# Second layers of expert pairs tile by tile, the last pair's one step later, and eight loads of shared rests

## The chip, the cores and the metric

One core of a Trainium2 chip runs the whole kernel. The metric is the device time of one execution in microseconds (us), here as the median of several runs. TensorE is called PE, VectorE DVE, ScalarE ACT, GpSimd POOL, SyncE SP.

## The reference

2048 rows (2 x 1024) of 256 numbers go through a gated cross attention and then through a mixture of experts:

```
x = x + tanh(g_xattn) * attention(layernorm(x), ctx)
y = layernorm(x)
shared = (sum over 2 of gelu(y @ sw1[s] + sb1[s]) @ sw2[s] + sb2[s]) / 2
gates = y @ router_w + router_b           # 8 experts, the top 2 of each row, softmax of the two
moe = sum over the 2 of prob * (gelu(y @ w1[e] + b1[e]) @ w2[e] + b2[e])     # 256 -> 512 -> 256
out = x + tanh(g_ffn) * (shared + moe)
```

Matrix products keep float32 accuracy: each operand is split into a rounded high part and a rest ("hi", "lo"), and three products are summed: hi x hi, hi x lo, lo x hi.

## The kernel before

Attention, routing and the first six of eight parts of the shared experts take the first 219 us of the span. Then the 4096 (row, expert) entries, sorted by expert, are worked through in 39 tiles of 128 rows (SLOT_TILES). Tiles 0 to 5 are single steps; tiles 6 to 29 are twelve pairs (DOUBLES), each of two tiles of one expert, worked as 256 rows; tiles 30 (SINGLE1) to 38 are single steps again. Last come the two parts of the shared experts that are left (EARLY and LAST) and the sum.

A tile goes through these stations:

- POOL gathers its rows (gather(s), into xsl) by a table of names that SP has loaded, and at the end scatters its result (scatter(s), y_tok). All POOL's DMAs stand in one written order. Behind the pairs it is gather(s + 2), scatter(s - 3) for s = 31, 32, ...; gather(s) also waits for xt_psum(s - 1).
- PE turns the rows (turn, L1458 and L1482), ACT copies the high part (turned, turned_wide), DVE makes the rest (xsT_lo, L2077 and L2089).
- PE does the first layer, here called hidden(s): single tiles 6 matmuls of 512 columns (L1550), pairs 24 of 256 (L1589).
- Single tiles: DVE copies the result out (hs, L2109), PE transposes it (L1574), ACT does the gelu (L1053) and the high part (hr_hi, L1057), DVE the rest (L2083). Pairs come out transposed already, in two halves of the 512 hidden units: gelus(h) (L1066), kept(h) (hr_hi, L1079) on ACT, half_left(h) (L2138) on DVE.
- PE does the second layer: give (12 matmuls, L1469), give_wide (24 matmuls, L1495). ACT takes it out, scaled by the weight of the expert (output, L1025, into ysl).

Every engine has its own written order. In double(s), PE does the first layer of the pair, turns the rows of the next pair, and does the second layer of the pair before: give_wide(s - 2). ACT does gelus(0), turned_wide for the next pair, kept(0), gelus(1), kept(1), and the outputs of tiles s - 2 and s - 1. DVE does b_cur (the bias column), xsT_lo for the next pair, half_left(0), a copy of next weights, half_left(1), another copy of weights. In the pair before the last, bias_weights(EARLY, LAST) stands at the end instead of weight copies.

kept(0) writes the first half of hr2_hi, which give_wide of the pair before reads, so it waits for half_used; kept(1) waits for ye_psum, the end of that give_wide:

```python
elif h == 0:
    act.wait_ge(half_used, s - DOUBLE0)
else:
    act.wait_ge(ye_psum, s)
```

hr_hi and hr_lo of the single tiles lie on the same words: tile 30's hr_hi on the first half of the last pair's. An output waits for the scatter that last used its ysl buffer (y_stored), two tiles earlier.

The rests of the shared experts' weights (sw_lo) were stored to DRAM to make room for w1_cur, the weights of the pairs. SP loads them back behind the last pair, in four pieces of 512 KB, in the loop that also loads the tables of names: at s = 35 to 38 it waits for xt_psum(s - 3), loads the table, and then loads a piece. The weights are wanted again at 353.6 us.

Of the kernel before, what the change touches and what calls it, by code (L numbers as in the profile page):

```python
# [16 lines left out]
F32 = mybir.dt.float32  # L17
# [51 lines left out]
def build(nc, x, ctx, g_xattn, g_ffn, g_x, b_x, g_c, b_c, Wq, Wk, Wv, Wo,  # L69
          router_w, router_b, w1, b1, w2, b2, sw1, sb1, sw2, sb2, out):  # L70
    st = ExitStack()
    with st:
# [376 lines left out]
        def _(sp):  # L449
# [65 lines left out]
            for s in range(SLOT_TILES):  # L515
                n = s % IN_FLIGHT
                if s >= IN_FLIGHT:
                    sp.wait_ge(xt_psum, s - IN_FLIGHT + 1)
                sp.load(regs[n], name_tile[0:1, entry(s):entry(s) + 1])
                row = sp.snap(regs[n], min_val=0, max_val=NAME_TILES - 1)  # L520
                sp.dma_start(table[:, s, :], name_tiles[at(row)].rearrange("a p c -> p (a c)")
                             ).then_inc(table_loaded[n], 16)
                n = s - (SLOT_TILES - BACK)
                if n >= 0:
                    sp.wait_ge(h_psum, SINGLE1 + n)
                    piece = slice(n * 2 * SW_WORDS // BACK, (n + 1) * 2 * SW_WORDS // BACK)
                    sp.dma_start(sw_s[1][:, piece].bitcast(F32), sw_lo_kept[:, piece]).then_inc(sw_moved, 16)

# [251 lines left out]
        def _(act):  # L780
# [253 lines left out]
            def step(s, par):  # L1034
                if s + 1 == DOUBLE0:
                    turned_wide(s + 1, 0)
                elif s + 1 < SLOT_TILES:
                    turned(s + 1, 1 - par)
                else:
                    act.wait_ge(h_psum, SLOT_TILES)  # L1040
                    columns(EARLY, late)
                if s == SINGLE1:
                    output(s - 2, 0)
                    output(s - 1, 1)
                elif s >= 2 and s != SINGLE1 + 1:
                    output(s - 2, par)
# [8 lines left out]
                last.then_inc(ht_raw, 1)  # L1055
                act.wait_ge(ht_raw, s + 1)
                nc.scalar.activation(hr_hi[:, par, :, :], hr[:, :, :], ACT.Copy).then_inc(ht_hi, 1)  # L1057

            def double(d, par, s, j):
# [28 lines left out]
                gelus(1)  # L1088
                kept(1)
                output(s - 2, 0)  # L1090
                output(s - 1, 1)
# [12 lines left out]
        def _(pe):  # L1104
# [381 lines left out]
            def give_wide(s, n):  # L1486

                e = expert(n)
                pe.wait_ge(ye_ready, s)
                for h in range(2):  # L1490
                    pe.wait_ge(ht_lo, s + (h + 1))
                    for t in range(2):
                        for i, (h_part, w_part) in enumerate(((hr2_hi, w2_s[0]), (hr2_hi, w2_s[1]), (hr2_lo, w2_s[0]))):
# [5 lines left out]
                        if h == 1:  # L1499
                            last.then_inc(ye_psum, 1)  # L1500
                    if h == 0:
                        last.then_inc(half_used, 2)

# [34 lines left out]
            def step(s, par):  # L1538
# [16 lines left out]
                if s + 1 < SLOT_TILES:  # L1555
# [3 lines left out]
                    else:  # L1559
                        turn(s + 1, 1 - par)  # L1560
                if s == SINGLE1:
                    give_wide(s - 2, 1)
                elif s >= 2 and s != SINGLE1 + 1:
                    if s == 2:
# [55 lines left out]
            give(SLOT_TILES - 2, SLOT_TILES % 2, SLOT_TILES - 2)  # L1620
            pe.wait_ge(sw_moved, 16 + 16 * BACK)
            hidden(EARLY, late, range(0, 1))
# [9 lines left out]
        def _(dve):  # L1632
# [468 lines left out]

            def step(s, par):

# [4 lines left out]
                dve.wait_ge(h_psum, s + 1)  # L2108
                nc.vector.tensor_copy(hs[:, :], bank[2 + par][:, :]).then_inc(h_ready, 1)  # L2109
                if s + 1 < SLOT_TILES:  # L2110
                    fetch(s + 1, entry(s + 1))
# [21 lines left out]
            def double(d, par, s, j):  # L2133
# [20 lines left out]
                if more:  # L2154
                    dve.wait_ge(h_psum, s + 2)
                    move_weights(par, 0)
                half_left(1)
                if more:
# [67 lines left out]
```

## Time and profile before

| | us |
|---|---|
| median of 3 runs | 384.3 (382.98 to 384.43) |
| the profiled execution: its time, its span | 384.16, 382.4 |
| PE busy | 372.3 (97%) |
| DVE, ACT, POOL busy | 282.1, 242.0, 220.1 |
| first and last second layer of a pair (L1495) | 250.4 and 322.1 |
| granted TensorE clock over the span | 1.000 |

Start times count from the start of the span. In a timeline a row gives start, duration, engine, line, operation, output and inputs, the count, and in brackets how long the engine was idle before it and what ended that. PE's matmuls overlap: a matmul of 256 columns is listed with 0.28 us, and the next starts 0.12 us later.

### The profile page before, as it was taken

How to read it: one execution, taken by the hardware profiler on the slowest of the kernel's cores; microseconds unless marked ns; L12 is line 12 of the kernel's file. 1: busy time of each engine (PE TensorE's matmuls, PEld its weight loads, DVE VectorE, ACT ScalarE, POOL GpSimd, SP SyncE). 2: the span in 40 equal slices, each digit the busy share in tenths (PEclk: the TensorE clock that was granted, in tenths of full speed). 3: DMA queues.
4: the chain of work that ended last, by engine and by line, in shares of the span. 5: the costliest groups of instructions: out<-in, count | busy, mean ns of one | idle time of the engine just before them, and what ended most of it. 6: DMA issues, size and time to landing. Idle time of an engine off the chain costs nothing.

```text
span 382.4 us, 8794 instructions
## 1 busy us (share of the span) xinstructions
PE 372.3 (97%) x2773; PEld 353.1 (92%) x2774; DVE 282.1 (74%) x612; ACT 242.0 (63%) x540; POOL 220.1 (58%) x262
## 2 busy tenths in 40 slices
PE   8999999999999999999999999999999998899996
PEld 7898889999999999999999989999999996779996
DVE  5798799978988988799899886555555653445486
ACT  2777545655664654887869857666666654667850
POOL 8367657688878764477782245566666564543100
PEclk9999999999999999999999999999999999999999
DMA  7990000001000058501950112222232323641397
GB/s 228 312 326 3 2 14 29 16 21 35 14 14 14 29 177 304 236 4 22 270 154 2 27 45 85 71 70 83 83 86 79 98 84 111 195 116 39 99 351 252
DMA packets 33263, 40.15 MB, mean 105 GB/s; under 512 B 9610, under 2 KB 26444, under 8 KB 33100
## 3 DMA queue, kind: packets, MB, share of 16 engines
q1 hardware_dynamic: 28384, 29.40, 24.8%
q0 software_dynamic: 4768, 10.28, 8.8%
q8 instruction: 19, 0.31, 0.4%
q14 instruction: 16, 0.13, 0.2%
q10 hardware_dynamic: 76, 0.02, 0.0%
HBM read 27.88 MB, written 11.68 MB: 103 GB/s over the span
## 4 chain that ended last, share of the span: by engine, by line
PE 85%; DMA 4%; DVE 3%; ACT 3%; issue 3%; POOL 2%; DVEq 0%; ACTq 0%; POOLq 0%
PE psum L1327 12%; PE psum L1350 12%; PE psum L1287 10%; PE psum L1243 9%; PE psum L1589 8%; PE psum L1495 6%; PE psum L1469 5%; PE psum L1550 4%; PE psum L1210 3%; DMA xsl<-y_rows,table 3%; PE psum L1129 2%; PE psum L1167 2%; PE psum L1191 2%; PE psum L1275 1%; PE psum L1482 1%
## 5 line engine op out<-in xcount | busy, mean ns | idle before, releaser
L739 POOL DMA_INDIRECT y_tok<-ysl,table x39 | 39.1, 1002 | 39.6 <-ACT ysl L1025 34.7
L732 POOL DMA_INDIRECT xsl<-y_rows,table x39 | 39.0, 1000 | 37.0 <-PE psum L1458 12.5
L705 POOL DMA_INDIRECT names<-named,pos x32 | 35.5, 1109 | 12.8 <-issue 8.2
L658 POOL TENSOR_TENSOR Eb<-Eb,rinv 128x512 f32<-128x512 f32 x32 | 33.5, 1066 | 13.1 <-DVE rinv L1801 13.1
L1066 ACT ACTIVATE hr<-psum,b_cur 128x256 f32<-128x256 f32 x48 | 20.2, 472 | 22.1 <-DVE b_cur L2094 12.3
L901 ACT ACTIVATE yTb<-psum 128x256 f32<-128x256 f32 x16 | 6.2, 385 | 42.6 <-PE psum L1307 42.6
L1589 PE MATMUL psum<-xsT_hi,w_cur 128*128 128x256 f32 x192 | 30.9, 283 | 0.0
L2138 DVE TENSOR_TENSOR hr_lo<-hr,hr_hi 128x512 fp32r<-128x512 f32 x24 | 16.6, 693 | 14.9 <-ACT hr_hi L1079 14.6
L641 POOL TENSOR_TENSOR half_sum<-Eb 128x512 f32<-128x512 f32 x16 | 20.6, 1288 | 12.1 <-ACT Eb L856 11.9
L1025 ACT ACTIVATE ysl<-psum,table 128x256 f32<-128x256 f32 x39 | 17.0, 467 | 16.1 <-PE psum L1469 11.3
L1589 PEld LDWEIGHTS psum<-xsT_hi,w_cur 128*128 128x128 f32 x192 | 26.5, 192 | 0.0
L1350 PE MATMUL psum<-sw_hi,early_hT_hi 128*128 128x256 f32 x96 | 24.2, 286 | 0.0
L2109 DVE COPY hs<-psum 128x512 f32<-128x512 f32 x15 | 10.4, 690 | 18.7 <-PE psum L1550 18.7
L936 ACT ACTIVATE early_stage<-psum,vec_col 128x256 f32<-128x256 f32 x48 | 20.0, 467 | 6.4 <-PE psum L1327 5.6
L1350 PE MATMUL psum<-sw_lo,early_hT_hi 128*128 128x256 f32 x96 | 23.8, 283 | 0.0
L866 ACT ACTIVATE pt_hi<-psum 128x512 fp32r<-128x512 f32 x32 | 17.7, 597 | 7.1 <-PE psum L1210 7.1
L1495 PE MATMUL psum<-w_hi,hr_hi 128*128 x96 | 20.4, 294 | 1.2 <-ACT ysl L1025 1.2
L2089 DVE TENSOR_TENSOR xsT_lo<-psum,xsT_hi 128x512 fp32r<-128x512 f32 x12 | 8.3, 692 | 17.8 <-ACT xsT_hi L1031 17.8
L1243 PE MATMUL psum<-A_hi,xn_hi 128*128 128x512 f32 (+1 forms) x64 | 21.4, 415 | 0.0
L1785 DVE TENSOR_TENSOR pt_lo<-psum,pt_hi 128x1024 fp32r<-128x1024 f32 x16 | 19.3, 1206 | 2.5 <-ACT pt_hi L866 2.2
L1748 DVE TENSOR_REDUCE mx<-psum 128x16 f32<-128x1024 f32 x16 | 19.4, 1212 | 1.7 <-PE psum L1243 1.7
L1243 PE MATMUL psum<-A_lo,xn_hi 128*128 128x512 f32 (+1 forms) x64 | 20.0, 393 | 0.0
(276 smaller groups left out, 1257.5 us busy)
## 6 DMA issues: line engine op xcount, KB each, us to landing
w_raw<-in_L_ffn_w SPq DMA_DIRECT2D x2, 4096.0 KB, 16.8
y_got<-y_tok SPq DMA_DIRECT2D x8, 512.0 KB, 8.1
xs_all<-in_x SPq DMA_DIRECT2D x4, 512.0 KB, 12.0
sw_raw<-in_L_ffn_sw SPq DMA_DIRECT2D x2, 1024.0 KB, 13.8
y_rows<-ybuf SPq DMA_DIRECT2D x16, 128.0 KB, 1.7
sw_lo_kept<-sw_lo SPq DMA_DIRECT2D x1, 2048.0 KB, 6.6
sw_lo<-sw_lo_kept SPq DMA_DIRECT2D x4, 512.0 KB, 4.4
out<-xs_all SPq DMA_DIRECT2D x3, 512.0 KB, 3.1
```

The lines of the kernel that those rows point to most:

```text
L641: nc.gpsimd.tensor_tensor(half_sum[:, :, :], Eb[q][:, :, 0:CTX // 2], Eb[q][:, :, CTX // 2:], ALU.add).then_inc(half_ready, 1)
L658: nc.gpsimd.tensor_tensor(Eb[q][:, heads, :], Eb[q][:, heads, :], rinv[:, q, heads].unsqueeze(2).broadcast_to([P, H // 2, CTX]), ALU.mult) ...
L705: nc.gpsimd.indirect_dma_start(names, bass.IndirectOffsetOnAxis(ap=pos[:, k, t:t + 1], axis=0), named[:, k, t, :], None).then_inc(scattere ...
L732: nc.gpsimd.indirect_dma_start(into[:, s % 2, :], None, y_rows, bass.IndirectOffsetOnAxis(ap=table[:, s, 0:1].bitcast(I32), axis=0)).then_ ...
L739: nc.gpsimd.indirect_dma_start(y_tok, bass.IndirectOffsetOnAxis(ap=table[:, s, 1:2].bitcast(I32), axis=0), ysl[:, s % 2, :], None).then_in ...
L1066: last = nc.scalar.activation(hr2[:, m, :], bank[2 + 2 * par + h][:, m * 2 * P:(m + 1) * 2 * P], ACT.Gelu, bias=b1_cur[:, par, 2 * h + m:2 ...
L1243: last = nc.tensor.matmul(bank[2 + 2 * par + g][:, :], x_part[:, par, k, :], a_part[:, at(b), k, g * BANK:(g + 1) * BANK].rearrange("p b n ...
L1287: last = nc.tensor.matmul(bank[1][:, 0:D], p_part[:, c, :], v_part[:, at(b), c, :].rearrange("p b n -> p (b n)"), start=start and n == 0, ...
L1327: last = nc.tensor.matmul(bank[2 + j][:, u * SUB:(u + 1) * SUB], w_part[:, s, k, hc * P:(hc + 1) * P], x_part[:, :, k, :], start=(n == 0), ...
L1350: last = nc.tensor.matmul(bank[acc + t][:, 0:D], h_part[:, m, t * P:(t + 1) * P], w_part[:, m, :], start=start and m == 2 * j and w_part i ...
L1495: last = nc.tensor.matmul(bank[6 + t][:, 0:D], h_part[:, m, t * P:(t + 1) * P], w_part[:, at(e), m, :].rearrange("p e n -> p (e n)"), star ...
L1589: last = nc.tensor.matmul(bank[2 + 2 * par + half][:, (m % 2) * 2 * P:(m % 2 + 1) * 2 * P], w1_cur[:, par, w_part, k, m * P:(m + 1) * P], ...
```

## The change

It has three parts.

1. give_wide does all 12 matmuls of its first tile, then all 12 of its second, in place of both tiles for the first half of the hidden units and then both for the second. half_used is raised behind the first half of the second tile.
2. give_wide of the last pair (tiles 28 and 29) moves from step 30 into step 31. The two outputs of the pair move with it, from ACT's step 30 into its step 31. ACT turns tile 31 in the last double already, ahead of the outputs of tiles 26 and 27, and waits for half_used before it writes hr_hi of tile 30. DVE takes the bias column and the hidden rows of tile 30 in the last double, between half_left(0) and half_left(1).
3. The rests of the shared weights come in eight loads of 256 KB: the first of each two as before, the second behind the transposes (ht_psum) of the same step.

```diff
--- before.py
+++ after.py
@@ SP @@
                 n = s - (SLOT_TILES - BACK)
                 if n >= 0:
-                    sp.wait_ge(h_psum, SINGLE1 + n)
-                    piece = slice(n * 2 * SW_WORDS // BACK, (n + 1) * 2 * SW_WORDS // BACK)
-                    sp.dma_start(sw_s[1][:, piece].bitcast(F32), sw_lo_kept[:, piece]).then_inc(sw_moved, 16)
+                    for i in range(2):
+                        if i == 0:
+                            sp.wait_ge(h_psum, SINGLE1 + n)
+                        else:
+                            sp.wait_ge(ht_psum, SINGLE1 + n + 1 - 2 * DOUBLES)
+                        piece = slice((2 * n + i) * SW_WORDS // BACK, (2 * n + i + 1) * SW_WORDS // BACK)
+                        sp.dma_start(sw_s[1][:, piece].bitcast(F32), sw_lo_kept[:, piece]).then_inc(sw_moved, 16)
@@ ACT, step @@
                 elif s + 1 < SLOT_TILES:
-                    turned(s + 1, 1 - par)
+                    if s != SINGLE1:
+                        turned(s + 1, 1 - par)
...
-                if s == SINGLE1:
-                    output(s - 2, 0)
-                    output(s - 1, 1)
-                elif s >= 2 and s != SINGLE1 + 1:
+                if s == SINGLE1 + 1:
+                    output(s - 3, 0)
+                    output(s - 2, 1)
+                elif s >= 2 and s != SINGLE1:
                     output(s - 2, par)
...
                 act.wait_ge(ht_raw, s + 1)
+                if s == SINGLE1:
+                    act.wait_ge(half_used, 2 * DOUBLES)
                 nc.scalar.activation(hr_hi[:, par, :, :], hr[:, :, :], ACT.Copy).then_inc(ht_hi, 1)
@@ ACT, double @@
                 kept(1)
+                if d == DOUBLES - 1:
+                    turned(SINGLE1 + 1, 1)
                 output(s - 2, 0)
                 output(s - 1, 1)
@@ PE, give_wide @@
-                for h in range(2):
-                    pe.wait_ge(ht_lo, s + (h + 1))
-                    for t in range(2):
+                for t in range(2):
+                    for h in range(2):
+                        if t == 0:
+                            pe.wait_ge(ht_lo, s + (h + 1))
                         for i, (h_part, w_part) in enumerate(((hr2_hi, w2_s[0]), (hr2_hi, w2_s[1]), (hr2_lo, w2_s[0]))):
...
                         if h == 1:
                             last.then_inc(ye_psum, 1)
-                    if h == 0:
-                        last.then_inc(half_used, 2)
+                        elif t == 1:
+                            last.then_inc(half_used, 2)
@@ PE, step @@
-                if s == SINGLE1:
-                    give_wide(s - 2, 1)
-                elif s >= 2 and s != SINGLE1 + 1:
+                if s == SINGLE1 + 1:
+                    give_wide(s - 3, 1)
+                elif s >= 2 and s != SINGLE1:
@@ PE, after the steps @@
-            pe.wait_ge(sw_moved, 16 + 16 * BACK)
+            pe.wait_ge(sw_moved, 16 + 32 * BACK)
@@ DVE @@
-            def step(s, par):
+            def bias_and_hidden(s, par):
...
                 nc.vector.tensor_copy(hs[:, :], bank[2 + par][:, :]).then_inc(h_ready, 1)
+
+            def step(s, par):
+
+                if s != SINGLE1:
+                    bias_and_hidden(s, par)
                 if s + 1 < SLOT_TILES:
@@ DVE, double @@
                     move_weights(par, 0)
+                if d == DOUBLES - 1:
+                    bias_and_hidden(SINGLE1, 0)
                 half_left(1)
```

## Rows read from the trace of the kernel before

**Rows 1.** Busy time by stage: us, busy us of each engine (instructions), clock, DMA

```profile
215.00:315.00 100.00, 99.87 (x803) 97.41 (x802) 61.70 (x112) 66.48 (x152) 58.43 (x59) 1.00 0.27 76
315.00:341.00 26.00, 21.96 (x144) 18.99 (x144) 11.36 (x26) 15.69 (x43) 13.00 (x14) 1.00 0.54 153
```

**Rows 2.** PE's waits from 215 us on: us in total, times, longest

```profile
PE psum L1550 <- DVE xsT_lo L2077: 1.3, 1, 1.3
PE psum L1495 <- ACT ysl L1025: 1.2, 1, 1.2
PE psum L1458 <- DMA xsl<-y_rows,table: 0.9, 1, 0.9
PE psum L1574 <- DVE hs L2109: 0.6, 1, 0.6
```

**Rows 3.** PE's timeline: start of hidden(30), and turn(34)

```profile
315.89 0.72 PE L1550 MATMUL psum<-w_hi,xsT_hi 128*128 x2
...
331.69 0.38 PE L1458 MATMUL psum<-ident,xsl 128*128 128x128 f32 x2
```

**Rows 4.** The chain that ended last, in order of time: start, us, what

```profile
307.10 1.45 PE psum L1495 x12
...
308.63 0.64 ACT hr_hi L1079
...
318.75 4.48 DMA y_tok<-ysl,table
...
325.22 0.63 ACT hr_hi L1057
...
326.74 1.65 PE psum L1550 x6
```

**Rows 5.** ACT's timeline in the pair loop: kept(0), the next gelus(0), kept(0)

```profile
289.96 0.63 ACT L1079 ACTIVATE hr_hi<-hr 128x512 fp32r<-128x512 f32 x1
...
294.70 0.84 ACT L1066 ACTIVATE hr<-psum,b_cur 128x256 f32<-128x256 f32 x2 [1.05 <-DVE b_cur L2094]
...
296.15 0.63 ACT L1079 ACTIVATE hr_hi<-hr 128x512 fp32r<-128x512 f32 x1
```

**Rows 6.** DVE's timeline: xsT_lo in the loop and of tile 30, last half_left(1)

```profile
296.13 0.69 DVE L2089 TENSOR_TENSOR xsT_lo<-psum,xsT_hi 128x512 fp32r<-128x512 f32 x1 [1.60 <-ACT xsT_hi L1031]
...
315.31 0.42 DVE L2077 TENSOR_TENSOR xsT_lo<-psum,xsT_hi 128x256 fp32r<-128x256 f32 x1 [1.18 <-ACT xsT_hi L1017]
...
318.15 0.69 DVE L2138 TENSOR_TENSOR hr_lo<-hr,hr_hi 128x512 fp32r<-128x512 f32 x1 [1.63 <-ACT hr_hi L1079]
```

**Rows 7.** PE's timeline: starts of two following pairs' first layers

```profile
291.20 0.64 PE L1589 MATMUL psum<-xsT_hi,w_cur 128*128 128x256 f32 x4
...
297.39 0.64 PE L1589 MATMUL psum<-xsT_hi,w_cur 128*128 128x256 f32 x4
```

**Rows 8.** POOL's timeline: scatter(28), then gather(34)

```profile
324.07 0.97 POOL L739 DMA_INDIRECT y_tok<-ysl,table  x1 [1.78 <-ACT ysl L1025]
325.35 0.98 POOL L732 DMA_INDIRECT xsl<-y_rows,table  x1 [0.31 <-issue]
```

**Rows 9.** Us to landing, issues at 325.1, 329.4, 332.9; last, 302.3 alone

```profile
sw_lo<-sw_lo_kept SPq DMA_DIRECT2D x1, 512.0 KB, 4.6
xsl<-y_rows,table POOLq DMA_INDIRECT x1, 4.7
...
sw_lo<-sw_lo_kept SPq DMA_DIRECT2D x1, 512.0 KB, 4.1
xsl<-y_rows,table POOLq DMA_INDIRECT x1, 4.6
...
sw_lo<-sw_lo_kept SPq DMA_DIRECT2D x1, 512.0 KB, 6.4
xsl<-y_rows,table POOLq DMA_INDIRECT x1, 6.8
...
xsl<-y_rows,table POOLq DMA_INDIRECT x1, 2.8
```

## Prediction

> **What bounds the kernel now.** I began with the busy time by stage. The reader is to see that TensorE (PE) is busy for all but 0.13 of the 100 us up to 315, and idle for 4.04 of the 26 us behind the last pair [rows 1]. The change touches just these two stretches. Then I asked who PE waited for: four waits, together 4.0 us, all from 317 to 340 [rows 2]. So the most that better cover can give back is 4.0 us; everything else that moves the time must come from PE being stopped where it now is not.
>
> Next came the transition, from hidden(30), the first layer of tile 30, at 315.89 to hidden(32) at 326.74: 10.85 us [rows 3, 4]. The last wait in it, 1.3 us [rows 2], is the one that the rest has to be read from: hidden(32) needs xsT_lo of tile 32, which stands behind ACT's gelu of tile 30, which stands behind output(28), which waits for the scatter of tile 26 to land, 4.48 us after its issue [rows 4]. ACT idles for nearly all of that.
>
> Last, the chain of work itself. It enters this stretch over "PE L1495 x12", twelve matmuls, and then "ACT hr_hi L1079" [rows 4]. That is the wait for half_used in kept(0). So the count of matmuls before half_used is on the path already.
>
> **Part 1, tile by tile.** The number of matmuls is the same (24 a pair), and twelve take 1.45 us [rows 4], 0.12 each. What moves is semaphores. ye_psum of the first tile comes after 12 in place of 18 matmuls, 0.72 us earlier; in the pair loop nobody uses that, since ACT comes to its two outputs only behind kept(1), which waits for both tiles. half_used comes after 18 in place of 12, 0.72 us later, since the first half of hr2_hi is read again for tile 1. kept(0) of the next pair waits for it, and behind kept(0) stand on ACT gelus(1), kept(1), both outputs, and on DVE both rests, a weight copy and the next b_cur.
>
> What is that worth? In the loop kept(0) starts at 289.96, the next pair's first gelu at 294.70 (it waits for b_cur, so nothing in between is slack), and xsT_lo runs from 296.13 for 0.69 us [rows 5, 6]. PE can start a hidden layer 0.16 us after xsT_lo has ended, as it does for tile 30 (315.31 + 0.42 to 315.89 [rows 3, 6]), so here at 296.98. It starts at 297.39, after a period of 6.19 us [rows 7]. The slack is 0.41 us. A delay of 0.72 leaves 0.31 us that PE must wait, and this chain, from half_used to the hidden layer that it lets go, spans two pairs. PE's own shift moves half_used again, so the excess repeats: 0.15 us a pair. kept(0) is delayed from pair 1 on; pairs 3 to 10 can feel it at their hidden layer: 8 x 0.15 = 1.2 us. With a slack of 0.72 it would cost nothing, with none twice that. The ACT loop alone has kept(0) every 6.19 us, at 289.96 and 296.15, the same as PE [rows 5], so it can't make up a delay.
>
> Behind pair 10 there is no slack: DVE builds the bias weights before b_cur of the last pair, xsT_lo of tile 30 starts at 315.31 and PE at 315.89, as soon as it has landed [rows 3, 6]. The full 0.72 us lands on PE there, less about 0.1 of pipelining. Some of the excesses fall in pairs 2 to 4, where PE waits a few tenths for rows anyway; I take 0.1 off. Part 1: +1.7 us at hidden(30). Bounds: 0.6 (only the place behind pair 10 pays) and 2.0.
>
> **Part 2, the last pair one step later.** It removes the cover of give_wide(28) from step 30 and puts it into step 31, adds turned(31) before ACT's outputs, and lets DVE copy the hidden rows of tile 30 before the last rest. Counted from hidden(30) at 0: the six matmuls are done at 1.65 [rows 4], and DVE copies hs until about 2.4 (0.7 us, as its other copies of 512 columns [rows 6]). The last rest of the pair, at 318.15 now [rows 6], is ready to start at 2.26 and starts right behind the copy; xsT_lo of tile 31 (0.42) follows and ends near 3.3; hidden(31) starts at 3.5. In between PE has only four transposes and idles over 1 us (now 1.2 before give_wide [rows 2]). give_wide(28) starts 1.6 later, at 5.1. Its 18th matmul ends 2.3 us on and releases half_used, and ACT's hr_hi copy of tile 30, for which the change adds a wait, starts at 7.55. This waiting instruction holds up turned(32), both outputs and gelu(31). From an hr_hi copy to the hidden layer two tiles on the trace has 325.22 to 326.74, 1.52 us [rows 4]. So hidden(32) starts at 9.1 in place of 10.85: -1.8 us. The stall of 1.3 becomes one of some 0.7, and the 4 us wait for the scatter is gone: it lands before output(28) wants it. Bounds: -1.3 (copies in DVE's new order cost more) and -2.1.
>
> What is late next is a transfer. On POOL, scatter(28) stands ahead of gather(34), 1.28 us apart [rows 8]. output(28) now comes behind the hr_hi copy and turned(32), from about 8.45 to 8.9; scatter(28) is issued at 9.2, gather(34) at 10.45, which is hidden(32) + 1.35; before, it is at -1.39. Its rows are wanted at turn(34), 4.95 us after hidden(32) [rows 3, 4]. It may take 3.6 us. Gathers took 2.8 us alone and 4.6 to 6.8 us beside a load of shared rests [rows 9]. The half load next to it is issued 0.3 before hidden(32), the following one at +2.7; I take 3.3 us and no stall. gather(35) may take 4.5 us and is near its limit too.
>
> **Part 3, eight loads.** Four more issues on SP, where the second of each two waits for the step's transposes. Queued behind it is the next table load, which waits for a later event of PE anyway: nothing. The same bytes go out over a step in place of at once. What this can touch is the 0.9 us that PE waits for gather(36) [rows 2], which took 6.8 us beside the fourth load (6.4) [rows 9]. Its allowance is 6.8 - 0.9 = 5.9 us. Half of the bytes now come about 1 us behind the gather. Between nothing and all 0.9, I take 0.4.
>
> The row shows each of three gathers landing within 0.5 us of the load beside it: 4.7 and 4.6, 4.6 and 4.1, 6.8 and 6.4 [rows 9]. The Trainium skill (DMA: Bandwidth & Descriptors, section Queues, rings and completion order) says that a transfer's semaphore write lands only after all earlier writes of the same DMA engine, across its queues. By that rule, with which these rows agree, a gather would land with a half load, and the whole 0.9 would go.
>
> **Sum.** Against the profiled execution's own 384.16 us (span 382.4 and 1.8 around it; the median of the three runs is 384.3, so the same): 384.16 + 1.7 - 1.8 - 0.4 = 383.7 us.
>
> **Rivals.** *The order costs nothing (B)*: PE sees no excess in the loop, for kept(0) may start sooner after half_used than I read, and the 0.6 behind pair 10 is all: 384.16 + 0.6 - 1.8 - 0.4 = 382.6, or 382.1 with all of part 3. For it: PE shows no idle in the loop now. Against: the spacing of kept(0) equals PE's. *The gather is late (C)*, the one that ends slower: gather(34), behind scatter(28), meets the loads 2b and 3a. With 4.7 us it stops PE for 1.1 us (384.8), with 6.8 us for 3.2 us (386.9). It decides the sign from 4.1 us on, and can be told from noise from 6.1 us on. For it: every gather beside a load took 4.6 or more. Against: those loads were whole. *The loads decide (D)*: gather(36) no longer stops PE at all, 383.2. *No effect of the tile order on the pairs, but the late hr_hi copy of tile 30 costs what the early ACT gains*: then part 2 is 0, and 384.16 + 1.7 - 0.4 = 385.5 (E). Against: the 1.52 us is read from rows.
>
> **Chances.** Forecast 0.48, B 0.18, C 0.12, D 0.17, E 0.05. A measurement tells about 0.5%, 1.9 us, from no change: below 382.4 faster, above 386.2 slower. Half of B falls below (0.09), and through the bounds some of D (0.05) and of the forecast (0.06): 0.2. Half of C falls above, and of E and the forecast a little: 0.1. Within: 0.7. The range goes from B with all of part 3 (382.1) to C with a gather of near 5.7 us (385.8).
>
> **What would show it.** Right: PE waits for xsT_lo (L2089) show up between pairs, some 0.3 us each second pair, and hidden(30) starts 1 to 2 us later; kept(0) starts after the 18th matmul. From hidden(30) to hidden(32) about 9.1 us; ACT waits some 3 us in front of the hr_hi copy of tile 30, for PE, and not for y_tok. Wrong: no idle in the loop (B); a wait of turn(34) or turn(35) for xsl (C); hidden(30) to hidden(32) above 10 (E). What would upset all of it is a stage outside of these 26 us that changes.

## The result and the profile after

The changed kernel takes 385.64 us in the median of 13 runs (384.94 to 387.74), the kernel before 384.01 in 13 runs beside it (382.98 to 386.83). The ratio is 1.0049, 95% interval 1.0031 to 1.0067: slower by 1.6 to 1.9 us where 383.7, a little faster, was forecast. The profiled execution took 387.11 us, span 385.4.

The busy time by stage, columns as in [rows 1]:

```profile
215.00:315.00 100.00, 98.15 (x768) 93.48 (x767) 59.34 (x102) 63.58 (x144) 56.99 (x56) 1.00 0.25 72
315.00:341.00 26.00, 23.67 (x162) 20.71 (x161) 12.33 (x33) 16.05 (x43) 14.60 (x15) 1.00 0.54 159
```

PE, idle for 0.13 us of these 100 before, now is for 1.85. Both are less than what is lost: a matmul is listed as busy for 0.27 us or more while the next one can start 0.12 us later, so short waits don't show as idle time. What follows goes by start times. PE's waits from 240 us on, for [rows 2]:

```profile
PE psum L1491 <- DMA xsl<-y_rows,table: 1.8, 5, 0.9
PE psum L1560 <- DVE xsT_lo L2087: 1.1, 3, 0.5
PE psum L1467 <- DMA xsl<-y_rows,table: 0.6, 1, 0.6
PE psum L1584 <- DVE hs L2119: 0.6, 1, 0.6
```

The waits of [rows 2] for ysl and the 1.3 for xsT_lo are gone, as foreseen. In their place stands a wait that no step of the forecast has: L1491, the turning of a pair's rows, waits five times for its gather, all inside the pair loop. PE's timeline, for [rows 3] (the first pair's hidden layer, then hidden(30), hidden(31), hidden(32), and turn(35)):

```profile
241.19 0.61 PE L1599 MATMUL psum<-xsT_hi,w_cur 128*128 128x256 f32 x3
...
320.91 0.72 PE L1560 MATMUL psum<-w_hi,xsT_hi 128*128 x2 [0.30 <-DVE xsT_lo L2087]
...
324.39 0.73 PE L1560 MATMUL psum<-w_hi,xsT_hi 128*128 x2 [0.38 <-DVE xsT_lo L2087]
...
330.01 0.72 PE L1560 MATMUL psum<-w_hi,xsT_hi 128*128 x2 [0.46 <-DVE xsT_lo L2087]
...
339.21 0.44 PE L1467 MATMUL psum<-ident,xsl 128*128 128x128 f32 x2 [0.59 <-DMA xsl<-y_rows,table]
```

Against the kernel before (its first pair at 240.91, hidden(30) at 315.89, hidden(32) at 326.74, hidden(38), the last, at 348.84; now 351.77), this gives a ledger of the two profiled executions: 0.28 us before the first pair (no part of the change is there), the twelve pairs 74.98 to 79.72 (+4.74), hidden(30) to hidden(32) 10.85 to 9.10 (-1.75), hidden(32) to hidden(38) 22.10 to 21.76 (-0.34). The sum is +2.93 of 3.0 in the spans; the medians lie 1.6 apart, since the profiled execution, 387.11 us, is the second slowest of its 13. The second and third items are as forecast (-1.8 and -0.4). The pair loop, put at +1.7 with the place behind it, is the miss.

**Which wait.** I cut each of the twelve pairs at PE's starts: first layer, turning (from the first transposition to the second layer; in the last pair it is turn(30)), second layer. Sums over the twelve, worked out from PE's timeline:

| profile | first layers | turnings | second layers | all |
|---|---|---|---|---|
| before | 34.66 | 4.66 | 35.66 | 74.98 |
| after | 34.89 | 8.35 | 36.48 | 79.72 |
| difference | +0.23 | +3.69 | +0.82 | +4.74 |

The forecast's chain over ACT and DVE ends in the wait for xsT_lo, seen at the end of the second layers: +0.82 us, and 0.36 of that is the last one, in front of hidden(30). The rest, 3.7 us, lies in the turnings, and has two causes. In six pairs (the fourth and the sixth to the tenth) the third transposition, the first of the second tile's rows, starts 0.04 or 0.05 us behind the landing of that tile's gather; they hold 3.1 us of it. In the others it is another wait, told below: 0.6 us.

**Which chain.** The chain that ended last goes through it. In order of time, from one kept(0) to the second layer two pairs later:

```profile
293.69 0.64 ACT hr_hi L1086
...
296.55 0.47 ACT ysl L1029
...
297.28 0.15 POOL y_tok L743
...
298.59 0.98 POOL y_tok L743
...
299.87 0.97 POOL xsl L736
...
301.15 3.32 DMA xsl<-y_rows,table
...
304.51 0.44 PE psum L1491 x2
304.95 2.99 PE psum L1505 x24
```

PE's timeline has the second layer's start 0.30 us behind the waiting transposition:

```profile
304.51 0.44 PE L1491 MATMUL psum<-ident,xsl 128*128 128x128 f32 x2 [0.31 <-DMA xsl<-y_rows,table]
304.81 0.51 PE L1505 MATMUL psum<-w_hi,hr_hi 128*128 x2
```

The 18th of the matmuls lets go the next kept(0) of this ring, at 307.31. So the ring is: kept(0), gelus(1), kept(1), the outputs (2.86 us), their scatter's start (0.73), four issues on POOL in their written order, scatter, scatter, gather, gather (3.87), the landing (3.32), the turning (0.48), and 18 matmuls to half_used and kept(0) (2.36): 13.62 us for two pairs, 6.8 a pair. The same steps in the kernel before, on ACT, POOL and PE:

```profile
292.82 0.82 ACT L1025 ACTIVATE ysl<-psum,table 128x256 f32<-128x256 f32 x2
```

```profile
293.55 1.00 POOL L739 DMA_INDIRECT y_tok<-ysl,table  x1 [1.37 <-ACT ysl L1025]
294.86 0.98 POOL L739 DMA_INDIRECT y_tok<-ysl,table  x1 [0.30 <-PE psum L1482]
296.14 0.98 POOL L732 DMA_INDIRECT xsl<-y_rows,table  x1 [0.30 <-issue]
297.42 0.96 POOL L732 DMA_INDIRECT xsl<-y_rows,table  x1 [0.30 <-issue]
```

```profile
300.27 0.60 PE L1482 MATMUL psum<-ident,xsl 128*128 128x128 f32 x4
300.63 0.48 PE L1495 MATMUL psum<-w_hi,hr_hi 128*128 x2
```

From kept(0) at 289.96 [rows 5] it is 2.86 + 0.73 + 3.87, the landing of 2.77, 0.08 to the first transposition, 0.36 to the second layer and 1.72 from its start to a kept(0): 12.38 us, two of PE's periods of 6.19. That sum alone says nothing of slack. The slack is where something lies ready: the second gather lands at 300.19, and PE comes to its rows, the third transposition, at 300.49 (0.11 us a transposition from 300.27). After a landing it could start within 0.04, so the ring had 0.26 us of slack in two pairs, and 0.27 to 0.35 in the six other pairs from the fifth to the eleventh. Kept(0) now comes 2.45 us after the second layer's start in place of 1.72, and a turning that had to wait takes 0.30 us from the third transposition to the second layer in place of 0.14. Estimated from these rows: 12.38 - 0.26 + 0.73 + 0.16 = 13.0 us, or 6.5 a pair, +0.31 on each. Five of the changed kernel's pairs, from the sixth on, took 6.52 to 6.83 us.

**A second ring, one pair long.** The outputs also let go PE's next second layer, which writes where they read (ye_ready). In the kernel before this ring is kept(0) to the outputs 2.86, the outputs 0.82, 0.23 from their end to the second layer (as where PE is listed as waiting for ysl in E14 and E15 below), and 1.72 to kept(0): 5.63 us against a period of 6.19. With 0.73 more it is 6.36, and binds: +0.17 a pair. It shows in the second profile of the changed kernel, E10, which took turns between the two rings. On ACT, then PE:

```profile
279.31 0.63 ACT L1086 ACTIVATE hr_hi<-hr 128x512 fp32r<-128x512 f32 x1 [0.73 <-PE psum L1505]
...
282.18 0.82 ACT L1029 ACTIVATE ysl<-psum,table 128x256 f32<-128x256 f32 x2
...
285.69 0.63 ACT L1086 ACTIVATE hr_hi<-hr 128x512 fp32r<-128x512 f32 x1 [0.31 <-PE psum L1505]
```

```profile
276.86 0.38 PE L1505 MATMUL psum<-w_hi,hr_hi 128*128 x1
...
283.23 0.38 PE L1505 MATMUL psum<-w_hi,hr_hi 128*128 x1
...
290.00 0.38 PE L1505 MATMUL psum<-w_hi,hr_hi 128*128 x1
```

From 276.86 to 283.23 it is 6.37 us, with the second layer 0.23 behind the outputs' end; from there to 290.00, where the gather binds, 6.77. The two together are 13.1, the ring over POOL. So that ring sets the pace, and without it this one would still cost 0.17 a pair.

**Why more than 6.5.** The second gather's landing grew from 2.8 to 3.2 and 3.3 us. On POOL and DVE, in the changed kernel:

```profile
293.14 0.98 POOL L736 DMA_INDIRECT xsl<-y_rows,table  x1 [0.30 <-issue]
...
294.42 1.46 POOL L736 DMA_INDIRECT xsl<-y_rows,table  x1 [0.30 <-issue]
```

```profile
294.35 0.69 DVE L2153 TENSOR_TENSOR hr_lo<-hr,hr_hi 128x512 fp32r<-128x512 f32 x1 [0.52 <-ACT hr_hi L1086]
294.96 0.69 DVE L2108 CAST w_cur<-w_hi 128x1024 fp32r x1
```

The gather's issue takes 1.46 us in place of 0.96 and ends 0.23 us behind the end of DVE's weight copy. In both profiles of the changed kernel the same holds for each of six second gathers that I compared (copies that end at 288.92, 295.65 and 302.39 here, gathers at 289.15, 295.88 and 302.63). So the later kept(0) also pushes the weight copy onto the gather, and that adds some 0.4 to 0.5 us to a turn of the ring: 13.0 becomes 13.5, where the changed kernel's pairs took 13.48 and 13.57 us two by two (second layers from 284.49 to 297.97, and from 291.24 to 304.81).

### The profile page after: what moved, and what is told of

Its sections match the earlier page's. It is cut to its first block, busy times and chain, and to the rows that moved or that the text cites. A ratio compares the mean times of both kernels' runs of the same rounds, so it can differ in the third digit from the quotient of the medians.

```text
span 385.4 us, 8799 instructions
## 1 busy us (share of the span) xinstructions
PE 375.2 (97%) x2773; PEld 353.4 (92%) x2774; DVE 282.0 (73%) x612; ACT 241.9 (63%) x540; POOL 221.5 (57%) x262
## 4 chain that ended last, share of the span: by engine, by line
PE 78%; issue 5%; POOL 4%; DMA 4%; ACT 3%; DVE 3%; DVEq 0%; ACTq 0%; POOLq 0%
PE psum L1336 12%; PE psum L1359 12%; PE psum L1296 10%; PE psum L1252 9%; PE psum L1478 5%; PE psum L1505 5%; DMA xsl<-y_rows,table 4%; PE psum L1599 4%; PE psum L1560 4%; PE psum L1219 3%; PE psum L1138 2%; PE psum L1176 2%; PE psum L1200 2%; POOL y_tok L743 2%; PE psum L1284 1%
## 5 line engine op out<-in xcount | busy, mean ns | idle before, releaser
L736 POOL DMA_INDIRECT xsl<-y_rows,table x39 | 40.8, 1047 | 33.1 <-PE psum L1359 11.7
L662 POOL TENSOR_TENSOR Eb<-Eb,rinv 128x512 f32<-128x512 f32 x32 | 33.5, 1065 | 13.1 <-DVE rinv L1811 13.1
L1505 PE MATMUL psum<-w_hi,hr_hi 128*128 x96 | 20.5, 295 | 0.0
L1086 ACT ACTIVATE hr_hi<-hr 128x512 fp32r<-128x512 f32 x24 | 15.2, 632 | 7.9 <-PE psum L1505 7.0
```

The source lines that it names most:

```text
L662: nc.gpsimd.tensor_tensor(Eb[q][:, heads, :], Eb[q][:, heads, :], rinv[:, q, heads].unsqueeze(2).broadcast_to([P, H // 2, CTX]), ALU.mult) ...
L736: nc.gpsimd.indirect_dma_start(into[:, s % 2, :], None, y_rows, bass.IndirectOffsetOnAxis(ap=table[:, s, 0:1].bitcast(I32), axis=0)).then_ ...
L1505: last = nc.tensor.matmul(bank[6 + t][:, 0:D], h_part[:, m, t * P:(t + 1) * P], w_part[:, at(e), m, :].rearrange("p e n -> p (e n)"), star ...
```

## The experiments

The four groups of runs in which the kernel before took 397 to 400 us, and the one (E9 to E12) in which it took 383.7 like at first, can't be compared by absolute times, so each ratio is to the kernel before within its own group. What differs at 397 us and more is not the landings: the few gathers in the pairs whose landing is recorded there (E3, E8) took 2.7 to 3.5 us, as at 384. It is ACT. In each of the six profiles at 384 us, in each of ten pairs, kept(0) starts 0.32 to 0.38 us behind the start of the matmul that lets it go. In the 14 profiles at the other level it starts 0.34 to 3.2 us behind. In E14 that matmul, the 17th, starts at 273.71 in one pair:

```profile
274.68 0.63 ACT L1079 ACTIVATE hr_hi<-hr 128x512 fp32r<-128x512 f32 x1 [1.86 <-PE psum L1495]
```

What holds ACT there no view names. Everything behind kept(0) comes later with it, and PE waits for outputs too. So these groups can show whether a later flag costs, but hardly by which ring it costs at 384 us. "Loop" is from the first pair's hidden layer to hidden(30), "transition" from hidden(30) to hidden(32).

**E1, E2, E3: the parts, and the flag alone.** E1 is the kernel before with the new order in give_wide alone. E2 is the changed kernel with the old order. E3 keeps the old order and only raises the flag later:

```
-                    if h == 0:
-                        last.then_inc(half_used, 2)
+                                if h == 1 and t == 0 and i == 2 and m == 2:
+                                    last.then_inc(half_used, 2)
```

> The kernel before with part 1 alone (tile by tile). In the changed kernel hidden(30) starts 5.0 us later than before. Theory P (ring over POOL): kept(0) -> outputs -> two scatters and two gathers on POOL -> landing -> turn two pairs later -> 18 matmuls -> kept(0) takes 13.5 us in place of 12.4, so part 1 alone puts hidden(30) at 320.5 to 321.1, PE waits at L1491 for xsl in most pairs, and with the transition as before (no gain of 1.8) the time is 387.5 to 389.5. Theory F (the forecast's chain over ACT and DVE alone): hidden(30) near 317.6, time near 385.9, waits for xsT_lo and not for xsl. Rival S: the loss comes from parts 2 or 3 or from a shift between runs; then this one is within 1 us of before.

> The changed kernel without part 1: second layers half by half again, parts 2 and 3 kept. All theories that put the loss on part 1: hidden(30) back at 315.7 to 316.3. The 12th matmul of give_wide(28) then releases the hr_hi copy of tile 30, 0.7 us sooner than the 18th, so hidden(32) follows hidden(30) by 8.4 us (9.1 in the changed kernel, 10.85 before). Time 381.3 to 382.3. Rival S: still above 384.

> The kernel before, half by half, where only half_used is raised later: on the 17th matmul in place of the 12th, 0.6 us later. Nothing else moves (ye_psum, the waits for ht_lo and the order of the matmuls are those of before). If the flag's time is the whole cause (theory P or F), the loss is about five sixths of that of the run with part 1 alone: by P hidden(30) at 319.5 to 321, time 386.5 to 389; by F 317.3 and 385.5. Rival Q: it is the order of the matmuls or the sooner wait for the second half's rest; then this one is the same as before, 384.0 within 0.5.

Measured, with the kernel before at 397.3: E1 400.4, ratio 1.0071 (1.003 to 1.0111); E2 396.1, 0.9973 (0.9931 to 1.0015); E3 400.2, 1.0068 (1.003 to 1.0106). Part 1 costs, and a flag raised five matmuls later costs as much with no matmul moved. The waits that theory P expected of E1 didn't come: from 240 to 340 us PE waits for ysl (5.5 us) and for hr_lo (1.4), and not for xsl.

**E4: POOL's order.** In the changed kernel the second scatter is issued behind the gathers:

```
-                for n in range(2):
-                    scatter(tile_of(d - 1) + n)
+                scatter(tile_of(d - 1))
...
+                scatter(tile_of(d - 1) + 1)
```

> The changed kernel, but in the pair loop POOL issues scatter, gather, gather, scatter in place of scatter, scatter, gather, gather: both gathers 1.28 us sooner, the second scatter 2.6 us later. Theory P: the ring over POOL gets 1.28 us shorter (13.5 to 12.2) and is no longer the bound; what is left is the chain over ACT and DVE, 12.7 for two pairs, so hidden(30) at 317 to 318 and the time 382.2 to 383.8; no waits for xsl at L1491. If the ring over POOL is not the cause, the time stays at 385.6 within 0.7. It can lose again if the late second scatter holds up the outputs (ACT waits for y_tok).

Measured 403.52 us, 1.0168 (1.0098 to 1.0239). A miss: PE no longer waits for xsl, as theory P had it, but the kernel is slower, and PE waits for ysl (8.7 us in eight waits of L1505). The reserve that was named doesn't explain it: of those ACT itself waits for a scatter (y_tok) in just two, 1.0 us together from 250 to 335 us. The first output comes 2.86 or 2.87 us behind kept(0) as ever, and kept(0) itself is late (0.4 to 2.9 us behind its matmul). Why this order is slower stays open.

**E5 to E8: the ring made shorter.** E5 is the changed kernel with its first output right behind kept(0); E6 the same on E2; E7 the same on the kernel before. E8 is the changed kernel with DVE's weight copy ahead of half_left(0).

```
                 kept(0)
+                output(s - 2, 0)
                 gelus(1)
                 kept(1)
...
-                output(s - 2, 0)
```

> The changed kernel, but in each pair ACT does the first of its two outputs right behind kept(0), where it waits for DVE for 0.8 us, in place of behind kept(1). Scatter, scatter, gather, gather on POOL then start about 1.3 us sooner after kept(0). Theory P (the ring kept(0), outputs, POOL's four issues, landing, turn, 18 matmuls binds): the ring falls from 13.5 to 12.2 us for two pairs, below PE's own 12.4; what is left is the chain over ACT and DVE, 12.7. The loop loses 1 to 2 us in place of 4.7, and the time is 2 to 4 us below the changed kernel's: about 1 to 1.5 us below the kernel before on the same chip. Theory F (only the chain over ACT and DVE): no gain from this; the output in front of gelus(1) could only cost. In the trace: PE no longer waits for xsl in the pair loop.

> Parts 2 and 3 without part 1, and the first output behind kept(0). Half by half the ring has 0.7 us more room, so the pair loop runs at PE's own 6.19 us a pair even where a transfer lands 1 us late. Hidden(30) to hidden(32) 8.4 to 8.6 us. Faster than the kernel before by 2 to 3 us where its loop has no idle, by more on a chip where transfers land later. The best of all versions if theory P holds.

> The kernel before with only the first output moved behind kept(0). Where the pair loop of before has no idle on PE: no change (within 0.3%). On a chip whose transfers land later, where the loop before already waits for rows or outputs: faster by what the loop waits, 2 to 6 us. If it is slower, an output ahead of gelus(1) costs the chain over ACT and DVE something.

> The changed kernel, but DVE copies the first half of the next weights (L2108) before half_left(0), not behind it. In the changed kernel the pair's second gather takes POOL 1.43 to 1.48 us, where it runs beside half_left(0) and this copy on DVE, and lands 3.2 to 3.3 us after issue; before it took 0.96 and 2.8. If DVE's two operations hold up POOL (theory P plus the port): the second gather is back at 1.0 us and lands 0.45 us sooner, the ring is 13.05 in place of 13.5, and the time falls by about 2 us below the changed kernel's. If the late landing comes from the DMA engines, or the ring is not the bound: within 0.5 us of the changed kernel.

Measured, with the kernel before at 398.46: E5 398.79, 1.0004 (0.9968 to 1.004); E6 393.29, 0.9865 (0.9823 to 0.9907); E7 394.94, 0.9898 (0.9837 to 0.9959); E8 399.46, 1.002 (0.9987 to 1.0054). An output moved ahead, nothing else, makes the kernel before 1% faster there, though it puts 0.4 us into the chain over ACT and DVE.

E5 missed what theory P expected, 1 to 1.5 us below the kernel before. PE's wait for xsl in the pairs is gone, but beside E6, which differs from it by part 1 alone, E5 is 5.5 us slower: with no wait for rows part 1 costs 1.4% all the same. PE waits for xsT_lo nine times (2.4 us) and for ysl four times (1.6). So at this level, with the ring over POOL out of the way, the loss goes over the others.

E8 isn't told apart from nothing, and the changed kernel itself wasn't in this group, so what the copy costs on POOL has no ratio of its own. Its trace does answer the question on POOL: in seven pairs in a row the second gather's issue takes 1.04 us, and of its four recorded landings three are at 2.8 and 2.9 us, the first at 3.45. Now the copy is the longer one, 0.88 to 0.90 us in place of 0.69, under the first gather's issue.

**E9 to E12: kernel before, changed kernel, part 2 alone, part 3 alone,** in a group where the kernel before takes 383.68 us.

> The kernel before, unchanged, for its profile beside the others of this call and for what the comparison calls nothing. Every theory: ratio 1.000, within 0.004. Hidden layer of the first pair to hidden(30) 75 us where the transfers land as in the first profile; 80 us if this chip is like that of the earlier runs, in which case the excess over 75 is the chip's and no theory's. hidden(30) to hidden(32): 10.8 us.

> The changed kernel, unchanged, beside its parts. Ratio 1.005 (1.003 to 1.007). If the loss is that of the ring kept(0), outputs, POOL, gather, turn_wide (theory P), the pair stretch is 4 to 6 us longer than that of the kernel before in this call; if it were the chain over ACT and DVE alone (theory F, the forecast's), 1 to 2 us longer. hidden(30) to hidden(32): 9.1 us in both.

> Part 2 alone (the last pair's second layer one step later, half by half as before). Both theories of the loss: the pair stretch is as long as in the kernel before, within 0.5 us, since half_used comes after the twelfth matmul. hidden(30) to hidden(32): the half_used of the last pair now comes 0.7 us earlier than in the changed kernel, so 8.4 in place of 9.1 us, against 10.8 before. That is 2.4 us less, ratio 0.994 (0.991 to 0.997). If the forecast of part 2 is wrong on its own: ratio 0.999 or more.

> Part 3 alone (eight half loads of the shared rests in place of four). The profiles of before and after have the wait for the gather of tile 36 at 0.89 and 0.59 us: ratio 0.999 (0.997 to 1.001), not told apart from nothing. If the loads did more than that, for good or ill, the ratio leaves 0.997 to 1.003 and the stretch behind hidden(32) shows it.

| | us | ratio (95%) | loop | transition |
|---|---|---|---|---|
| E9 before | 383.75 | 0.999 (0.9961 to 1.0019) | 75.04 | 10.90 |
| E10 changed | 385.63 | 1.0047 (1.0025 to 1.007) | 79.00 | 9.10 |
| E11 part 2 alone | 381.19 | 0.9924 (0.9896 to 0.9953) | 74.95 | 8.40 |
| E12 part 3 alone | 381.80 | 0.9941 (0.992 to 0.9961) | 74.96 | 9.76 |

The loop is 75.0 us without part 1, whatever else is changed, and 79.0 or 79.7 with it. In E10 the turnings hold 2.37 us of the 3.96 more than E9's (1.5 in the four pairs whose rows landed just before, 0.9 in those that waited for outputs), the second layers 1.16, the first layers 0.42. There the second gathers issue in 0.96 or 1.10 us in turn, and four of its pairs in the middle take 6.56 to 6.62 us, which is the ring's 13.0 us for two pairs and the 0.14 by which every other second gather is held.

E11 is faster by 2.5 us. Its hr_hi copy of tile 30, the waiting one, comes 1.78 us behind the second layer's start in place of 2.49, since half_used comes after the 12th matmul:

```profile
320.21 0.48 PE L1500 MATMUL psum<-w_hi,hr_hi 128*128 x2
...
321.99 0.63 ACT L1060 ACTIVATE hr_hi<-hr 128x512 fp32r<-128x512 f32 x1 [2.60 <-PE psum L1500]
...
323.52 0.71 PE L1555 MATMUL psum<-w_hi,xsT_hi 128*128 x2
```

E12 is the surprise: 1.9 us, where nothing measurable was expected. Its chain that ended last, for the 4.48 of [rows 4]:

```profile
319.00 3.40 DMA y_tok<-ysl,table
...
325.90 1.63 PE psum L1554 x6
```

The first load of shared rests, half as large, is issued 0.1 us before the scatter of tile 26, and the scatter lands in 3.4 us in place of 4.48. ACT's output(28), which waits for it, and hidden(32) come 1.1 us sooner. Behind hidden(32) no gather stops PE: 20.86 us to hidden(38), in place of 22.10 in the first profile of the kernel before, where gather(36) does.

The 22.54 of E9 is something else. PE waits for no gather there, but its clock fell. PE's 2.5 us of waits for output and xsT_lo lie from 317 to 327 us in both profiles of the kernel before; in E9's, three stretches from 324 us on (columns as in [rows 1]):

```profile
324.00:326.00 2.00, 0.66 (x4) 0.42 (x4) 0.56 (x3) 1.51 (x5) 1.44 (x2) 1.00 0.40 103
326.00:327.00 1.00, 0.84 (x2) 0.75 (x3) 0.68 (x3) 0.28 (x2) 0.95 (x1) 0.57 0.73 156
327.00:328.00 1.00, 1.00 (x3) 0.74 (x3) 0.00 (x0) 0.97 (x5) 0.44 (x1) 0.50 0.78 283
```

A granted clock of 0.50 is the lower of the two levels, 1.2 GHz; hidden(32) took 2.72 us in place of 1.49. In this group 9 of the 31 runs of the kernel before had a mean clock of 0.996 or less (384.8 us in the median, the others 383.4), and none of the 32 runs of E10, E11 and E12. That is consistent with part of the gain of parts 2 and 3 being a clock that no longer falls behind this idle time; no run separates it.

**E13 to E16: order, flag, output first and no order, once more.** E13 is E1's kernel, E14 E3's, E15 E5's, E16 E2's.

> Part 1 alone once more, for its size beside the next three. Theory P (ring over POOL): first pair's hidden layer to hidden(30) 79 to 80 us where the kernel before has 75.0, each two pairs about 13.4 us in place of 12.4; ratio 1.011 to 1.014 where the chip takes 384 us for the kernel before. Theory F (ACT and DVE chain with a slack of 0.41 us): 76.2 to 77 us, ratio 1.003 to 1.005.

> The kernel before with half_used raised five matmuls later, nothing else: first pair's hidden to hidden(30) within 0.6 us of that of part 1 alone by both theories, and the ratio within 0.003 of it. If the order of the matmuls does harm by itself (their weight loads, the psum banks), this one stays near 75 us and 1.000.

> The changed kernel with its pair's first output right behind kept(0), which takes about 1.3 us out of the ring over POOL and puts 0.4 us into the chain over ACT and DVE. Theory P: first pair's hidden to hidden(30) falls from 79 to 77 us or less (what is left is the other chain), no wait of PE for xsl in the pair loop, ratio to the kernel before 0.996 to 1.000 in place of 1.005. Theory F: it rises to 81 us or more, ratio 1.008 or more.

> Parts 2 and 3 without the order. If both take the same wait (the scatter of tile 26 that output(28) stood behind): hidden(30) to hidden(32) 8.4 us as with part 2 alone, no wait for a gather behind it, and a ratio of 0.992 (0.990 to 0.994), like part 2 alone. If they were worth their sum: 0.987. If the half loads harm part 2 (earlier, 9.0 in place of 8.4 us from hidden(30) to hidden(32) was seen on a slower chip): 0.994.

The kernel before took 399.73 us in this group, so the numbers expected for 384 us don't apply, and the runs are read against each other, with the loop cut as above. The turnings end where the second layer starts, so waits for outputs (ysl) are in them too:

| | us | ratio (95%) | first layers | turnings | second layers | loop |
|---|---|---|---|---|---|---|
| E13 order | 402.70 | 1.006 (1.0021 to 1.01) | 35.31 | 15.47 | 38.74 | 89.52 |
| E14 flag | 400.74 | 1.0019 (0.9975 to 1.0064) | 35.20 | 14.12 | 37.45 | 86.77 |
| E15 changed, output first | 398.83 | 0.9966 (0.9931 to 1.0001) | 35.61 | 11.43 | 39.86 | 86.90 |
| E16 parts 2 and 3 | 400.14 | 1.0032 (0.9982 to 1.0082) | 35.22 | 10.95 | 36.83 | 83.00 |

The later flag alone lengthens the loop by 3.8 us against E16, 3.2 of it in the turnings. With the output moved ahead the turnings are 4.0 us shorter than E13's and the second layers 1.1 longer. These are single profiled executions: the same kernels had loops of 86.84 (E1), 80.84 (E2), 83.70 (E5) and 86.81 (E18), so 2 to 3 us lie between two profiles of one kernel. E13's loop also holds a second layer of 4.35 us in place of 2.85 (at 281.87, granted clock 0.54), behind a stretch in which PE was busy for 2.13 of 4 us. What PE waited for from 240 to 340 us, in E14 and then E15:

```profile
PE psum L1495 <- ACT ysl L1025: 6.7, 6, 2.5
PE psum L1482 <- DMA xsl<-y_rows,table: 1.5, 4, 0.7
PE psum L1589 <- DVE xsT_lo L2089: 0.6, 1, 0.6
...
```

```profile
PE psum L1505 <- ACT ysl L1029: 5.1, 7, 1.3
PE psum L1599 <- DVE xsT_lo L2099: 1.9, 7, 0.4
...
```

The wait for xsl is gone, and the wait that the forecast spoke of, xsT_lo, has come in: seven times, up to 0.4 us. But in both the largest wait is that for ysl. With the ring over POOL out of the way the two others bind, kept(0) over the outputs to the second layer above all.

Parts 2 and 3 without part 1 (E2, E16) show no gain at this level, though the transition is shorter, 9.0 us. Behind it, hidden(32) to hidden(38) takes 22.4 and 22.5 us there, and 20.9 in E1, E7, E13 and E14, which have neither part: in E2 PE waits once for 1.2 us for the hidden rows (hs), and in E16 for 1.4. Part of what the transition gains is lost there.

**E17, E18: flag alone and output first, a third time.**

> The kernel before with half_used raised five matmuls later and nothing else. Where the kernel before takes 384 us: first pair's hidden layer to hidden(30) 79 to 80 us if the flag's time is all of part 1's loss (the changed kernel has 79.0 and 79.7, the kernel before 75.0), ratio 1.010 to 1.014; 75 to 76 us and 1.000 to 1.003 if the order itself were the cause. Kept(0) would come after the seventeenth matmul, 0.6 us later than before, in both.

> The changed kernel with the first output of its pair right behind kept(0). Where the kernel before takes 384 us: theory P (ring over POOL) 77 us or less from the first pair's hidden layer to hidden(30) and no wait of PE for xsl there, ratio 0.996 to 1.000; theory F (ACT and DVE chain) 81 us or more, ratio 1.008 or more. On a chip where it takes 397 us or more: ratio 0.997 to 1.000, as twice before.

Again a group at 399.18 us. E17: 401.02, 1.0027 (0.998 to 1.0073); E18: 398.54, 0.9968 (0.9927 to 1.0009). E18 repeats E15. E17 repeats E14: over its three groups the flag alone is at 1.0068, 1.0019 and 1.0027, the order alone, in two, at 1.0071 and 1.006. The intervals overlap; whether the order has a small cost beside the flag's isn't settled.

## Why the prediction was wrong

**Part 1, the step that failed.** "The slack is 0.41 us" is right for the chain that it was read from, and half_used does come 0.72 us later (0.73 measured). But I looked for who waits for kept(0) on ACT and DVE only and stopped at the outputs: "behind kept(0) stand on ACT gelus(1), kept(1), both outputs". I didn't follow the outputs to POOL, where two scatters stand ahead of the gathers that PE needs two pairs later, nor to PE, whose next second layer waits for them. The spacing of POOL's issues is in [rows 8], and I used it for tile 34 alone. The ring over POOL had a slack of 0.26 us in two pairs, against 0.73 of delay: 0.31 us a pair, and 0.56 with the gather held by DVE's copy, where pairs 7 to 10 took 0.51 to 0.60 more. The ring over the outputs had 0.56 in one pair, and would cost 0.17. "The ACT loop alone has kept(0) every 6.19 us, the same as PE" read an equal period as a lack of slack; in a steady loop every engine has that period, and a ring's slack is read where something lies ready before it is used.

The forecast's bounds of 0.6 to 2.0 hold only its own chain, which did cost 0.8 to 1.2 (second layers), with 0.36 behind pair 10 in place of 0.6. Together: +4.0 and +4.7 in two profiles, against +1.7.

**Shown and not shown.** That part 1 makes the loss is shown by E9 to E12, all in one group. That the time of the flag is enough is shown in E3; E14 and E17 lean the same way, with intervals that include no change. The same again with the output first: E5 against E6, in one group, 1.0004 against 0.9865.

Which way the loss goes at 384 us is read from the two profiles of the changed kernel: the chain that ended last, the transpositions that start 0.04 or 0.05 us behind a landing in six and in four pairs, and the two rings' lengths, which come out within 0.1 us. No experiment shows it. Where the kernel before takes 384 us neither the flag alone nor the output first was measured. At 397 us and more the wait for xsl does go with the output first, but the loss by part 1 doesn't, and E15's loop, 2.6 us shorter than E13's, holds 1.5 us less of a fallen clock and differs in parts 2 and 3 as well.

**Part 2.** Right in place and size: -1.75 and -1.80 us against -1.8. ACT waits in front of the hr_hi copy for PE, not for y_tok:

```profile
328.50 0.63 ACT L1064 ACTIVATE hr_hi<-hr 128x512 fp32r<-128x512 f32 x1 [3.31 <-PE psum L1505]
```

Of the transition's gain part 1 takes back 0.7 us: 8.40 us in E11. E2 and E16, with the old order, had 9.00 and 9.04 all the same, while E6 had 8.39; what holds the copy there I can't say; kept(0) in the pairs is late at that level too.

**Part 3.** The gain inside the change was near what I took (0.34 against 0.4), though the wait moved: gather(36) no longer stops PE, gather(35) does, for 0.59 us, after 5.0 us to landing. In E10 no gather does. Alone it is worth 1.9 us, since it also hastens the scatter of tile 26. Part 2 takes the wait for that scatter out of the transition altogether, so the 1.1 us that part 3 gains there can't be had twice; what it gains behind hidden(32) might add. The two parts without part 1 weren't measured at 384 us. I had weighed the loads against the gathers and left out the scatter beside the first load.

**The rivals.** B (the order costs nothing) is wrong by sign. C (gather(34) late) didn't happen: it was issued at 331.61, hidden(32) + 1.60 where I had + 1.35, and landed in 2.8 us. D is seen in E10. E, near in its total of 385.5, is wrong in its mechanism.

**Best versions.** Part 2 alone, 0.9924, is faster than both kernels at 384 us, and parts 2 and 3 with the output first, 0.9865, in a group at 398. The latter wasn't measured at 384.

## What to carry to other kernels

Before a semaphore is raised later, follow each engine queued behind its waiter to where PE waits again, with the DMA queues and their landings as links, and look in each ring for the place where something lies ready before it is used: that time is its slack. A loop without idle time may have several rings with little of it, and the shortest slack isn't always on the engines looked at first. What two edits gain from the same wait can't be had twice. A test of a ring has to be run where that ring binds. A version made of the parts that gain is worth a run of its own.

## What the runs showed of the hardware that I had not expected

**POOL's gather and DVE's weight copy exclude each other.** In the six cases, and in three of the kernel before (at 259.56, 265.96 and 297.42), a gather that was under way when the copy from w_hi began ended 0.22 to 0.24 us behind the copy's end: 0.96 us with a copy that ended 0.72 after the gather's start (the gather at 297.42), 1.09 and 1.10 with 0.86 and 0.87 (E10), 1.43 to 1.48 with 1.20 to 1.24. Where the copy began late in the gather, it was the copy that took longer (0.78 us at 308.59 in place of 0.69) and the gather 0.96. The Trainium skill (SBUF — State Buffer, section SBUF: two separate sides) has DVE and GpSimd share a port pair as an exclusive lock, held for a whole instruction, so that GpSimd can't write descriptors meanwhile. These rows agree in that one holds up the other. They don't show that the first to start keeps the lock: the gather at 294.42 began 0.54 us before the copy, and it was the gather that took longer. Which operands of the copy take the lock no run here tells. Nor is the weight copy all that holds POOL: the scatter at 326.63 in the kernel before took 1.39 us in place of 0.97, beside no weight copy.

**The same kernel at two levels.** The kernel before took 384 us in two groups and 397 to 400 in four, with the granted clock at 0.98 to 1.00 in the profiled runs of both; chip 14 showed both levels. What was seen to differ in the pairs is how late ACT starts kept(0), above. The parts are worth other amounts there: parts 2 and 3 together were at 0.9973 and 1.0032, while each alone was at 0.992 to 0.994 in the 384 us group. A change that moves waits between engines wants its ratio from both.
